# A recommendation model's interaction and MLP on one core: wide products of high and low halves, and who adds, splits and subtracts

## The reference

```
dots  = einsum('bfd,bgd->bfg', x, x)               # 27 x 27 Gram matrix of a sample
pairs = dots[:, tril_i, tril_j]                    # its 351 entries below the diagonal
h = concatenate([dense, pairs, zero], axis=1)      # 128 + 351 + 1 = 480 wide
for w, b in (w0,b0), (w1,b1), (w2,b2), (w3,b3):    # 1024, 1024, 512, 256 wide
    h = relu(h @ w.T + b)
y = h @ w_out.T + b_out                            # one number per sample
```

## Time and profile before

| | us |
|---|---|
| median of 3 runs | 530.62 (528.19 to 531.23) |
| the profiled execution | 531.61 |
| its span, first to last instruction | 529.8 |
| PE busy / PEld busy | 497.5 / 486.9 |
| DVE / ACT / POOL busy | 289.7 / 333.4 / 260.6 |

### The profile page before, as it was taken

How to read it: one execution, slowest core, us unless ns; L and a number is a source line. 1 busy time by engine, 2 the same in 40 slices (tenths; PEclk the granted TensorE clock), 3 DMA queues, 4 the chain that set the end, 5 groups by cost and what they waited for, 6 DMA issues and landing times.

```text
span 529.8 us, 13442 instructions
## 1 busy us (share of the span) xinstructions
PE 497.5 (94%) x4073; PEld 486.9 (92%) x4073; DVE 289.7 (55%) x646; ACT 333.4 (63%) x844; POOL 260.6 (49%) x467
## 2 busy tenths in 40 slices
PE   6876987799999999999999999999999999999996
PEld 6866976699999899998999999998999999999996
DVE  2673787457762667446853676357753676232101
ACT  3543789746984578737984588647883698433112
POOL 2710356413875357634865277625764387524221
PEclk9997999999999999999999999999999999999999
DMA  8997677544563566447663656266653662210000
GB/s 228 237 333 137 225 120 115 99 93 79 88 109 70 101 113 96 68 98 123 94 106 67 107 98 109 41 126 111 104 80 78 116 108 41 51 46 1 1 1 0
DMA packets 281054, 53.23 MB, mean 100 GB/s; under 512 B 265126, under 2 KB 279230, under 8 KB 281022
## 3 DMA queue, kind: packets, MB, share of 16 engines
q1 hardware_dynamic: 279090, 52.22, 51.9%
q10 hardware_dynamic: 1932, 0.61, 0.5%
HBM read 45.71 MB, written 7.09 MB: 100 GB/s over the span
## 4 chain that ended last, share of the span: by engine, by line
PE 58%; DMA 11%; POOL 9%; issue 7%; SPq 7%; ACT 4%; DVE 3%; POOLq 0%; DVEq 0%; ACTq 0%
PE acc L729 46%; PE gram_ps L692 6%; DMA blocks<-grams 5%; ACT parts L820 3%; POOL parts L566 3%; SPq L412 3%; DMA early_rows<-in_r_bottom_output_dram 2%; POOL grams L573 2%; SPq L407 2%; POOL h_a L581 2%; PE gram_ps L644 2%; DMA rows<-in_r_bottom_output_dram 2%; PE gram_ps L673 2%; POOL h_b L581 1%; DMA pairs<-blocks 1%
## 5 line engine op out<-in xcount | busy, mean ns | idle before, releaser
L729 PE MATMUL acc<-h_a,w_hi 128*128 128x256 f32 x1152 | 214.7, 285 | 4.3 <-POOL h_a L581 3.0
L729 PEld LDWEIGHTS acc<-h_a,w_hi 128*128 128x128 f32 x1152 | 178.0, 191 | 8.0 <-POOL h_a L581 5.7
L820 ACT ACTIVATE parts<-gram_ps 27x216 f32<-27x216 f32 x448 | 152.9, 341 | 23.4 <-PE gram_ps L692 13.9
L836 ACT ACTIVATE h_full<-acc,small_t 128x256 f32<-128x256 f32 x172 | 81.4, 474 | 132.2 <-PE acc L729 128.9
L729 PE MATMUL acc<-h_a,w_lo 128*128 128x256 f32 x576 | 162.6, 282 | 0.0
L581 POOL TENSOR_TENSOR h_a<-h_full,h_a 128x256 fp32r<-128x256 f32 x96 | 72.1, 751 | 139.2 <-DVE h_a L955 139.2
L729 PEld LDWEIGHTS acc<-h_a,w_lo 128*128 128x128 f32 x576 | 109.8, 191 | 0.0
L729 PE MATMUL acc<-h_b,w_hi 128*128 128x256 f32 x512 | 93.9, 284 | 0.0
L729 PE MATMUL acc<-x,w_hi 128*128 128x256 f32 x480 | 90.3, 287 | 0.0
L581 POOL TENSOR_TENSOR h_b<-h_full,h_b 128x256 fp32r<-128x256 f32 x64 | 47.3, 739 | 81.6 <-DVE h_b L955 81.6
L566 POOL TENSOR_TENSOR parts<-parts 128x128 f32<-128x128 f32 x112 | 82.5, 737 | 5.8 <-ACT parts L820 5.3
(11 more groups left out here) (59 smaller groups left out, 439.2 us busy)
## 6 DMA issues: line engine op xcount, KB each, us to landing
rows<-in_r_bottom_output_dram SPq DMA_DIRECT2D x444, 64.0 KB, 2.0
blocks<-grams SPq DMA_DIRECT2D x30, 216.0 KB, 3.8
w_raw<-in_L_rec_w_dram SPq DMA_DIRECT2D x6, 1024.0 KB, 7.2
early_rows<-in_r_bottom_output_dram SPq DMA_DIRECT2D x12, 224.0 KB, 6.2
stage_pairs<-in_L_rec_w_dram SPq DMA_DIRECT2D x1, 1408.0 KB, 10.2
w_raw<-in_L_rec_w_dram SPq DMA_DIRECT2D x2, 512.0 KB, 8.8
mlp_rows<-r_bottom_mlp_output_dram SPq DMA_DIRECT2D x8, 128.0 KB, 2.2
pairs<-blocks SPq DMA_DIRECT2D x8, 126.0 KB
```

Source lines behind the costliest of these rows:

```text
L729: last = nc.tensor.matmul(acc_slot(c, slot), weight(wp, layer, m, k), in_tile(layer, k, xp), start=(k == 0 and n == 0), stop=(k == K_TILES ...
L820: last = nc.scalar.activation(parts[quad_of(s), u % 2, :, :, 0:FEATS], gram_found(u, s), ACT.Copy)
L836: nc.scalar.activation(h_full[:, slot % 2, :], acc_slot(c, slot), ACT.Relu, bias=small_t[:, slot:slot + 1]).then_inc(drained, 1)
```

## The change

The accumulator of a tile now takes 512 columns, a whole bank. w_hi multiplies the high and low parts in one matmul of 512 columns; the left half of the bank receives the product with the high part, the right half that with the low part. w_lo by the high part is a matmul of 256 columns into the left half. ACT moves the right half with the bias into h_full, now without the relu (semaphore `low_moved`). DVE adds the left half to it (`add_halves`), and this now gives `drained`. DVE alone splits: a maximum with 0 into the high part, and an instruction that takes the maximum with 0 and subtracts the high part. `weigh` takes its relu itself, with one more instruction for its second tile. In exchange POOL makes `turned_lo`, ahead of `add_parts` in its order, and DVE no longer does.

```diff
         def acc_slot(c, slot):
             if isinstance(c, int) and c == 0 and 2 <= slot < EARLY_TILES:
-                return (turned_ps if slot < 4 else gram_ps)[:, slot - 2, 0:CHUNK]
-            return acc[:, slot % ACC_RING, 0:CHUNK]
+                return (turned_ps if slot < 4 else gram_ps)[:, slot - 2, :]
+            return acc[:, slot % ACC_RING, :]
 ...
 # GpSimd
-            def split_low(c, layer, m):
-                slot, h = slot_of(layer, m), h_b if layer == 1 else h_a
-                pool.wait_ge(high_done, split_count(c, slot))
-                nc.gpsimd.tensor_tensor(h[:, m, 1, :], h_full[:, slot % 2, :], h[:, m, 0, :].bitcast(F32),
-                                        ALU.subtract).then_inc(split_done, 1)
+            def turned_lo(d, u):
+                pool.wait_ge(xt_hi_done, (d - 1) * UNITS + u + 1)
+                nc.gpsimd.tensor_tensor(xt_part(u, 1), raw_cols(u), xt_part(u, 0).bitcast(F32),
+                                        ALU.subtract).then_inc(xt_done, 1)
 ...
 # TensorE
-                    for n, (wp, xp) in enumerate(((w_hi, 0), (w_hi, 1), (w_lo, 0))):
-                        last = nc.tensor.matmul(acc_slot(c, slot), weight(wp, layer, m, k), in_tile(layer, k, xp),
-                                                start=(k == 0 and n == 0), stop=(k == K_TILES[layer] - 1 and n == 2))
+                    found, src = acc_slot(c, slot), in_tile(layer, k)
+                    nc.tensor.matmul(found, weight(w_hi, layer, m, k), src.rearrange("p h n -> p (h n)"),
+                                     start=(k == 0), stop=False)
+                    last = nc.tensor.matmul(found[:, 0:CHUNK], weight(w_lo, layer, m, k), src[:, 0, :],
+                                            start=False, stop=(k == K_TILES[layer] - 1))
 ...
 # ScalarE, drain
-                nc.scalar.activation(h_full[:, slot % 2, :], acc_slot(c, slot), ACT.Relu,
-                                     bias=small_t[:, slot:slot + 1]).then_inc(drained, 1)
+                nc.scalar.activation(h_full[:, slot % 2, :], acc_slot(c, slot)[:, CHUNK:], ACT.Identity,
+                                     bias=small_t[:, slot:slot + 1]).then_inc(low_moved, 1)
 ...
 # VectorE
-            def turned_lo(d, u):
-                dve.wait_ge(xt_hi_done, (d - 1) * UNITS + u + 1)
-                nc.vector.tensor_tensor(xt_part(u, 1), raw_cols(u), xt_part(u, 0).bitcast(F32),
-                                        ALU.subtract).then_inc(xt_done, 1)
+            def add_halves(c, layer, m):
+                slot = slot_of(layer, m)
+                full = h_full[:, slot % 2, :]
+                dve.wait_ge(low_moved, slot_count(c, slot))
+                nc.vector.tensor_tensor(full, acc_slot(c, slot)[:, 0:CHUNK], full, ALU.add).then_inc(drained, 1)
-            def split_high(c, layer, m):
+            def split(c, layer, m):
                 slot, h = slot_of(layer, m), h_b if layer == 1 else h_a
+                full, high = h_full[:, slot % 2, :], h[:, m, 0, :]
                 dve.wait_ge(drained, slot_count(c, slot))
-                nc.vector.tensor_copy(h[:, m, 0, :], h_full[:, slot % 2, :]).then_inc(high_done, 1)
+                nc.vector.tensor_scalar(high, full, 0.0, None, ALU.max).then_inc(high_done, 1)
+                dve.wait_ge(high_done, split_count(c, slot))
+                nc.vector.scalar_tensor_tensor(h[:, m, 1, :], full, 0.0, high.bitcast(F32),
+                                               ALU.max, ALU.subtract).then_inc(split_done, 1)
 ...
 # VectorE, weigh
-                    nc.vector.tensor_scalar(weighted[:], full, w, None, ALU.mult).then_inc(weighed, 1)
+                    nc.vector.tensor_scalar(weighted[:], full, 0.0, w, ALU.max, ALU.mult).then_inc(weighed, 1)
 ...
-                nc.vector.scalar_tensor_tensor(weighted[:], full, w, weighted[:], ALU.mult,
-                                               ALU.add).then_inc(weighed, 1)
+                nc.vector.tensor_scalar(full, full, 0.0, w, ALU.max, ALU.mult).then_inc(scaled, 1)
+                dve.wait_ge(scaled, c + 1)
+                nc.vector.tensor_tensor(weighted[:], full, weighted[:], ALU.add).then_inc(weighed, 1)
```

More of the change, by code:

```diff
@@ L308, in dlrm_program @@
         filled = sem("filled")
+        low_moved = sem("low_moved")
         drained = sem("drained")
@@ L314, in dlrm_program @@
         mlp_done = sem("mlp_done")
+        scaled = sem("scaled")
         weighed = sem("weighed")
@@ L342, in acc_slot, with in_tile @@
             if isinstance(c, int) and c == 0 and 2 <= slot < EARLY_TILES:
-                return (turned_ps if slot < 4 else gram_ps)[:, slot - 2, 0:CHUNK]
-            return acc[:, slot % ACC_RING, 0:CHUNK]
+                return (turned_ps if slot < 4 else gram_ps)[:, slot - 2, :]
+            return acc[:, slot % ACC_RING, :]
         mlp_bank = turned_ps[:, 0, 0:CHUNK]
         out_bank = turned_ps[0:1, 1, 0:CHUNK]
-        def in_tile(layer, k, part):
+        def in_tile(layer, k):
             src = x0 if layer == 0 else h_b if layer == 2 else h_a
-            return src[:, k, part, :]
+            return src[:, k]
         def weight(part, layer, m, k):
@@ L575, in add_parts @@
                     parts[:, u % 2, 0, :, 0:FEATS], low_t[:, u % 2, :, 0:FEATS], ALU.add).then_inc(grams_done, 1)
-            def split_low(c, layer, m):
-                slot, h = slot_of(layer, m), h_b if layer == 1 else h_a
-                pool.wait_ge(high_done, split_count(c, slot))
-                nc.gpsimd.tensor_tensor(h[:, m, 1, :], h_full[:, slot % 2, :], h[:, m, 0, :].bitcast(F32),
-                                        ALU.subtract).then_inc(split_done, 1)
+            def turned_lo(d, u):
+                pool.wait_ge(xt_hi_done, (d - 1) * UNITS + u + 1)
+                nc.gpsimd.tensor_tensor(xt_part(u, 1), raw_cols(u), xt_part(u, 0).bitcast(F32),
+                                        ALU.subtract).then_inc(xt_done, 1)
             def chunk(c):
                 for step in steps_of(c):
[L586 to L589, removed]
+                    if step[0] == "turn":
+                        turned_lo(c + step[1], step[2])
                     elif step[0] == "sum":
@@ L990, in chunk @@
                         if k1 == K_TILES[layer]:
+                            add_halves(c, layer, m)
                             if layer < 3:
-                                split_high(c, layer, m)
+                                split(c, layer, m)
                             else:
@@ L996, in chunk @@
                         turn_raw(c + step[1], step[2])
-                    elif step[0] == "turn":
-                        turned_lo(c + step[1], step[2])
                     elif step[0] == "sum":
```

## The result

The changed kernel takes 563.24 us (median of 5 runs, 560.95 to 566.69) against 529.84 us before (5 runs). The ratio is 1.062, 95% interval [1.058, 1.066]: slower by 33 us, where 10 were forecast, and above the forecast's range.

The account below looks back on a forecast made before the run. PE's pace was taken as the bound on average, the tile-emptying engines near theirs in layer 0. Chunks 1 to 6 +7.8, chunk 7 -0.4, chunk 0 +2.2: +9.6 on 531.61 = 541.2, median 540 us, range 515 to 557.

Parts of the forecast that it names:

- the rival taken as likeliest: Layer 0: VectorE and the shared port set the pace; 540 us, own range 524 to 558, chance 0.50.
- The matmuls: PE's k-steps: 13.3 ns fixed per instruction saved, 360 to 346.7 ns; 1.8 us a chunk, 14.5 us in all.
- the per-column rival (C): PE's matmuls: the extra time is per column, so the wide matmul gives nothing; 551 us, chance 0.12.
- the 325 ns one (D): PE's matmuls: a k-step takes 325 ns, a further 18 us saved in layers 1 to 3; 522 us, chance 0.13.
- Start of a chunk: Next chunk's first product waits for the accumulator behind pairs_lo and the add: stall 0.4 to 0.8, taken as 0.6 us.
- Layer 0: VectorE late for tile 7: stall 0.65 us, with port waits 2.5 us a chunk (bounds 0.65 and 4.7).
- 5 × 0.37 = 1.85: Layer 0: VectorE's port waits over five tiles at 0.37 us each, 1.85 us in all.
- In layers 1 and 2 VectorE catches up: Layers 1 and 2: with 8 k-steps a tile (2.8 us), VectorE makes up its lateness from layer 0.
- The port wait as an average: Layer 0: two VectorE operations a tile wait for GpSimd, 0.62 × 0.3 × 2 = 0.37 us (bounds 0 and 0.8).
- Chunk 0: First chunk: -1.3 from matmuls, +2.5 around the early tiles, +1.0 for the units; +2.2 us in sum.
- +1.0 (bounds 0 and 5): Chunk 0, 70 to 101 us: ScalarE bounds at 2.15 us a unit, GpSimd has 2.0 plus port waits; +1.0 us.
- Rival B: Layer 0: VectorE keeps up, port waits fall in ScalarE's shadow, no stall; 518 us, chance 0.25.

Follow-up runs that it names:

- e1_wide: The kernel before with only the wide matmul (one of 512 columns, one of 256), right half left out of the sum: 523.86 us, ratio 0.990.
- e7_narrow: The changed kernel with three matmuls of 256 columns as before, the product counted twice: 567.75 us, ratio 1.072.
- e8_third: The changed kernel with a third accumulator, used from slot 8 of chunk 0 on: 567.12 us, ratio 1.067.
- e5_short: The changed kernel with GpSimd's turned_lo over 108 of 432 columns, the other low parts of x left zero: 541.40 us, ratio 1.026.
- e10_writes: The changed kernel with turned_lo over 108 of 432 columns, followed by three GpSimd memsets over the other groups: 545.42 us, ratio 1.027.
- e6_chunk0: The changed kernel with turned_lo of the 16 units run inside chunk 0 given back to VectorE: 560.39 us, ratio 1.059.
- e2_add: The kernel before with only VectorE's add put before the accumulator's release, matmuls narrow, product counted twice: 550.05 us, ratio 1.041.
- e4_wide_add: The kernel before with wide matmuls and the add, but without the swap of VectorE's and GpSimd's work and without the relu: 544.66 us, ratio 1.030.
- e3_swap: The kernel before with only the swap: VectorE subtracts for h's low parts, GpSimd makes turned_lo; full result: 531.08 us, ratio 0.999.
- e9_later: The kernel before with only the swap (VectorE subtracts, GpSimd makes turned_lo), in chunks 1 to 7 only; full result: 526.83 us, ratio 0.991.

## Why the prediction was wrong

The direction, and the rival taken as likeliest (VectorE and the shared port set layer 0), were right. The size was not: +9.6 forecast, +31.1 between the profiled spans. Of the 21.5 us between them, chunks 1 to 6 have 14.3 and chunk 0 8.4; chunk 7 and the start give 1.2 back. In a steady chunk (forecast, measured): layer 0 +2.1, +2.6; layer 1 -0.85, +0.84; layer 2 -0.4, -0.3; last layer and change +0.5, +0.6.

- **The matmuls: right in themselves, off in the sum.** 346.7 ns a k-step undisturbed, so neither the per-column rival (C) nor the 325 ns one (D) held. The Trainium skill (TensorE: Matmul & The Clock Gate, Back-to-back issue gap) gives N/2.4 + 2.5 ns for the gap of an isolated matmul, which is 216 ns for 512 columns; the trace has 230 to 233 in this stream. But 14.5 us was never on the path in full: the wide matmul is worth 6 alone (e1_wide) and 4.5 here (e7_narrow), since a faster PE meets the splits and the units sooner (e1_wide's wait at 298.86 shows it for the splits; for the units it is argued).
- **Start of a chunk: right.** A stall of 0.6 was forecast at the next chunk's first product; PE waits 0.48 there (before 261.94). Counted as even was a wait inside layer 3: it is now 1.12 (before 259.19) where before had 0.7 in two pieces. The last layer and the change together take 0.58 more.
- **Layer 0: nearly right, with two errors that half cancel.** "5 × 0.37 = 1.85" of port waits was too low. VectorE went back to back from its first add (264.37 in the chunk above) to its sixth (276.10): 11.73 us. Five times 1.20 and the three hooks that lie there at 0.86 are 8.58, so the port took 3.15. In exchange one hook less than counted lay in between (-0.86); that VectorE could begin 2.43 after PE's first product was as counted. 2.5 + 1.3 - 0.86 is 2.9, and the measured stall is 3.0 (16.62 less 14.03, plus the 0.4 that the products save).
- **"In layers 1 and 2 VectorE catches up": the step that failed in the steady chunks.** It is nearly true behind the first tile, but layer 1's first tile needs the split of the last tile of layer 0, and VectorE comes there as late as it has become: PE waits 1.21 us in one piece. I had priced the release of the accumulators only, not this second place where the same lateness is paid. Forecast for layer 1: -0.85; measured +0.84; e8_third shows that taking the first price away raises the second.
- **The port wait as an average: the false assumption behind it.** I took the rest of a GpSimd operation at a random moment, 0.37 us a tile. The phase is not random: a unit puts turned_lo just ahead of L960 (0.23 us in the rows above). Where they meet, the price is 0.8 us, my upper bound, time after time; in layer 0 of a steady chunk that is five of eight tiles, and the two operations of a tile are longer by 0.69 us on average. e5_short and e10_writes price the whole at 22 and 18 us. The Trainium skill (SBUF — State Buffer, Who interferes with whom) says that a VectorE instruction with two SBUF inputs contends with a GpSimd one that reads SBUF, "not with one that only writes it"; e5_short against e10_writes agrees. "Exactly two of a tile's three operations wait" holds in kind: the maximum ends 0.15 us after the GpSimd operation that it starts behind, and the add is never held. But the two pay unequally, 0.16 and 0.53 us on average in layer 0, since the maximum mostly meets the short L575.
- **Chunk 0: mis-sized term, +2.2 forecast, +10.6 measured.** "+1.0 (bounds 0 and 5)" for the units was the poorest choice: I had GpSimd at 2.0 us plus port waits in a unit of 2.15 and chose near the lower bound. turned_lo on GpSimd is 4.6 of the 10.6 (e6_chunk0, read from one trace each), the add some 4 (chunk 0 takes 94.6 in e2_add and 95.1 in e4_wide_add). That the add costs so much because the units' and the tiles' steps share VectorE's order is argued, not shown; some 2 us are assigned to nothing.
- **The add in front of the release: the largest part, and forecast only inside other terms.** Alone it costs 20 us (e2_add), in a kernel whose VectorE was 55% busy and where no operation with two SBUF inputs is new: in layer 0 (0.6 a chunk), at the change to layer 1 (0.4), in the last layer and the change of chunk (0.9), and in chunk 0 (3.8). At the changes it is taken for the delay; in layer 0, where VectorE is then busy 13.1 of 14.6 us, its load may count too, and no run parts the two.
- **Rival B** (VectorE keeps up, 518) needed a tile's three operations under 1.1 us; beside a turned_lo they take 1.98 (339.97 to 341.95 above).

In sum: before 530, the wide matmul -6, the add +20 (together 545, as e4_wide_add shows), the swap on top about +19. The swap's cost exists only with the add, which moves the two-input operation behind the start of turned_lo: without the add VectorE's subtraction took 0.49 to 0.57 on average (e3_swap), with it 0.81 to 0.88.

What stays open: why e9_later's chunk 0 is 1.5 us shorter than before's, and what part of chunk 0's growth is the lower granted clock (0.91 to 0.97 in its layer 1 in the changed kernel and in seven of the ten experiments, e9_later among them, against 1.00 before) and what part the waits. Why the clock fell behind four of e8_third's six equal gaps and not behind the other two is open too.

## What to carry to other kernels

An instruction put in front of the release of a double buffer costs more than its duration: price it at every place where the next consumer stands ready (buffer release, layer change, chunk change), and do not count an engine's slack later as cover. Where two engines exclude each other at a port, look at what releases what: if one triggers the other, they can meet at the same phase each time, and the price of a meeting is then near the upper bound, not the mean. A saving on the bounding engine shrinks when it is nearly bound elsewhere: here 14.5 us by the sum was 6. And when a wait is moved rather than removed, look at the clock behind it before judging the buffer: in e8_third the buffer gained 0.65 us a chunk and the clock took more.

## What the runs showed of the hardware

- VectorE's split operation with two inputs in SBUF takes 0.43 us alone, 0.52 to 0.69 where it starts behind the start of a GpSimd subtraction of 108 columns (0.48 to 0.49 on average over all), and 1.20 to 1.39 behind one of 432. It ends 0.28 to 0.29 us after the GpSimd operation that holds it up, in all 79 cases of the changed kernel. GpSimd's memsets did not hold it up.
- The maximum, with one input in SBUF, takes 0.29 us alone and up to 1.21 behind a turned_lo, and ends 0.15 us after it. The add, with one input in PSUM, takes at most 0.43 whatever GpSimd does.
- A matmul of 512 columns repeats after 230 to 233 ns and one of 256 after 117 to 120: 17 to 20 and 10 to 13 ns over the columns at 2.4 GHz (213.3 and 106.7). The pair is 26.7 ns over, as much as two times the 13.3 of the forecast.
- After a PE gap of 2.1 us, with PE busy 0.86 us of the 3 around it, the granted clock fell to 0.77 and 0.69 in the next windows in four chunks of e8_third, and stayed at 1.00 in two. Gaps of 1.2 us at the same place in the changed kernel left it at 1.00 six times, while in e4_wide_add one gap of 1.21 (before 427.49), with one of 0.44 behind it, was followed by 0.73 and 0.71 (428 to 430, 430 to 434).
